# Routing tail and experts of a four-layer cross-attention stack: powers computed earlier, three scatters under way, two blocks made one

## Chip, cores and metric

The kernel runs on one core of one Trainium2 chip. The metric is the device time of one execution in microseconds; before the change it is 3072.48 us, the median of three runs (3069.31 to 3073.73).

## What is computed

A stack of four layers works on `x` (32 batches of 112 tokens, width 256, f32) with a context of 32 x 375 rows. Each layer adds a gated attention over the context and a gated second part: mixture of experts, a searched network, a ternary product, a routed layer. The change touches only the first layer:

```python
x = x + tanh(g_xattn[0]) * attention0(layernorm(x), ctx, pad_mask)
x = x + tanh(g_ffn[0])   * mixture0(layernorm(x))
# mixture0, on N = 3584 tokens, 8 experts of capacity 1024:
probs = softmax(x @ Wr);  w_topk, e_topk = top_k(probs, 2)
pos   = place of each (token, choice) in its expert's queue, in token order
buf   = zeros(8, 1024, 256).at[e_flat, pos].set(x_rep, mode='drop')
h     = rms(buf, norm_w);  buf_out = (gelu(h @ Wg) * (h @ Wu)) @ Wd + buf
combined = x + sum over 2 choices of w_topk * buf_out[e, pos]
fout  = gelu(rms(x) @ fWg) * (rms(x) @ fWu) @ fWd + x     # shared, small
out   = where(a choice overflowed its expert, fout, combined)
```

## The kernel before, in words

`first_attention` (L209) is one block: five instruction streams, one for each engine, that meet at a barrier when it ends. It walks the 32 batches in a software pipeline; batches are also four groups of eight (`G = 8`) for the routing. For each group TensorE makes the router's logits, VectorE multiplies them by the tokens' inverse size (`token_shift`, L1329, which waits for `r_invs_done`), ScalarE takes the exponential, VectorE picks the two best experts (`token_pick`), TensorE counts places (`token_places`, L1368), and VectorE turns them into row numbers (`token_rows`, L1381, which raises `put_ready`). GpSimd then writes the group's rows into a queue in HBM by 16 indirect transfers (`token_scatter`, L1398), each of up to 112 rows of 1 KB.

The inverse sizes come from GpSimd: `token_half_scales` (L1229), `token_sizes` (L1238) and `token_inverses` (L1248), which are powers of the variances.

After the last attention batch comes the tail, in four functions. `shared_scatters` (L1451) is GpSimd's: the scatters of groups 2 and 3 (`LAST - 1` and `LAST`), with a wait for the landing of all so far after each fourth, and group 3's sizes after the fourth scatter of group 2, its inverses after the eighth. `shared_vectors` (L1467), `shared_scalars` and `shared_products` (L1550) are the shared expert for all eight half groups (`gate_and_up(n)`, `gelu(n)`, `hide(n)`, `down(n)`, `add_shared(n)`), with group 3's routing written into that order by hand: VectorE does `hide(1)`, `add_shared(0)`, `token_shift(3)`, `token_pick(3)`, `hide(2)`, `add_shared(1)`, `token_rows(3)`, and so on; ScalarE takes group 3's exponential ahead of `gelu(2)`; TensorE does `route_rows`, `gate_and_up(2)`, `down(1)`, `gate_and_up(3)`, `token_places(3)`, `down(2)`, and so on. The last `add_shared` raises `added` to 32.

Then the block ends: every engine drains, they meet, the semaphores are cleared. `run_experts` (L1630) is the next block: 16 units of 512 queue rows, two to an expert. Weights of expert 0 are there by then; the slots of experts 1 and 2 lie where the attention's tiles lay. SyncE loads the rows of units 0 and 1 (512 KB each), then six weight transfers of 512 KB (experts 1 and 2), then goes on unit by unit. GpSimd starts five small loads. TensorE transposes unit 0's rows as soon as they are in, and from there products of 128x512 follow each other.

Once the experts are done, `gathered_attention` (the second layer's attention, which also fetches the experts' output rows) and the rest follow; nothing of them is changed.

Of the kernel before, what the change touches and what calls it, by code (L numbers as in the profile page):

```python
# [13 lines left out]
P = 128  # L14
# [40 lines left out]
def row(v):  # L55

    return v.rearrange("(a n) -> a n", a=1)
# [151 lines left out]
def first_attention(k, m, t):  # L209
# [4 lines left out]
    with nc.cleanup_on_exit():  # L214
        w = Fields()
# [35 lines left out]
        ctx_loaded = [sem(nc, f"ctx{j}_loaded") for j in range(NB)]  # L251
# [5 lines left out]
        shared_storage(k, q, w.pad, s)  # L257

        with nc.Block() as block:
            @block.sync  # L260
            def _(sp):
                opening_loads(k, w, o, sp)
                sp.wait_ge(o.s["zeros_ready"], 1)
                for j in range(CT, B):
                    sp.wait_ge(s["scores_done"], j - CT + 1)
                    sp.dma_start(w.ctx_t[:, j % CT, :, :], k.ctx_t_dram[j]).then_inc(w.ctx_t_loaded[j % CT], 16)
                    if j == 2 * CT:
                        for t, src in ((m.f_norm[:, :], (k.inputs["L0_ffn_f_norm"])), (m.fwg[:, :, :], k.inputs["L0_ffn_fWg"]),
                                       (m.fwu[:, :, :], k.inputs["L0_ffn_fWu"]), (m.fwd[:, :], k.inputs["L0_ffn_fWd"]),
                                       (m.wr[:, :, :], k.inputs["L0_ffn_Wr"])):  # L270
                            sp.dma_start(t, src).then_inc(m.s["shared_loaded"], 16)
# [9 lines left out]
                for j in range(NB):  # L281
                    sp.wait_ge(ctx_loaded[j], 16 * (B // NB))

            @block.gpsimd
            def _(pool):
# [68 lines left out]
                shared_scatters(k, m, t, pool)  # L354

            @block.vector
            def _(dve):
# [101 lines left out]
                shared_vectors(k, m, t, q, dve, PLACES)  # L459

            @block.scalar
            def _(act):
# [76 lines left out]
                shared_scalars(k, t, q, act)  # L539

            @block.tensor
            def _(pe):
# [62 lines left out]
                def attend(j):  # L605
                    u = j % 2
                    if j < NB:
                        pe.wait_ge(k.ctx_first[j], 16)
                    else:
                        pe.wait_ge(ctx_loaded[j % NB], 16 * (j // NB))  # L610
# [48 lines left out]
                shared_products(k, m, t, q, pe, PLACES)  # L659

# [596 lines left out]
def routing_storage(k, w, net):  # L1257
# [48 lines left out]
    t.scattered = [sem(nc, f"scattered{g}") for g in range(B // G)]  # L1306
# [91 lines left out]
def token_scatter(k, t, pool, g, n):  # L1398

    j, r = divmod(n, TOP_K)  # L1400
    if n == 0:
        pool.wait_ge(t.s["put_ready"], g + 1)
    pool.indirect_dma_start(k.queue[:, :], bass.IndirectOffsetOnAxis(ap=t.put_at[:, g, r, j:j + 1], axis=0), t.xr[g][:, j, :], None,
                            bounds_check=ROWS - 1, oob_is_err=False).then_inc(t.scattered[g], 16)
# [43 lines left out]
LAST = B // G - 1  # L1448


def shared_scatters(k, w, t, pool):  # L1451

    token_half_scales(k, w, pool, GH * (LAST + 1) - 1)
    for g in (LAST - 1, LAST):
        for n in range(G * TOP_K):
            token_scatter(k, t, pool, g, n)
# [173 lines left out]
def run_experts(k, w, net):  # L1630

    nc = k.nc
    UNITS_E = CAPACITY // UR
    N = E * UNITS_E
    with nc.cleanup_on_exit():
        rows = sb(nc, "rows", [P, 2, TILES, D], F32)
        rows_t = sb(nc, "rows_t", [P, 2, DC, UR], F32)
        gated = sb(nc, "gated", [P, 2, UR], F32)
        hidden = sb(nc, "hidden", [P, 2, FC, UR], F32)
        out = sb(nc, "out", [P, 2, TILES, D], F32)  # L1640
        rows_in = [sem(nc, f"rows{u}_in") for u in range(N)]
        rows_out = [sem(nc, f"rows{u}_out") for u in range(N)]
        names = "transposed rows_copied gate_done gated_done up_done hidden_done down_done out_copied"
        s = {n: sem(nc, n) for n in names.split()}
        RT, GATE, UP, DOWN = 0, 2, 4, 6

        with nc.Block() as block:
            @block.sync
            def _(sp):
                for u in range(N + 2):  # L1650
                    if u < N:
                        if u >= 2:
                            sp.wait_ge(s["transposed"], u - 1)
                        sp.dma_start(rows[:, u % 2, :, :], k.queue[u * UR:(u + 1) * UR, :].rearrange("(p t) d -> p t d", p=P)).then_inc(rows_in[u], 16)
# [3 lines left out]
                    if u >= 2:  # L1658
                        sp.wait_ge(s["out_copied"], 2 * (u - 1))
                        sp.dma_start(k.outputs[(u - 2) * UR:(u - 1) * UR, :].rearrange("(p t) d -> p t d", p=P), out[:, u % 2, :, :]).then_inc(rows_out[u - 2], 16)  # L1660
                    e, last = divmod(u - 1 - UNITS_E, UNITS_E)
                    if last == 0 and 0 <= e < E - EXPERT_RING:
                        sp.wait_ge(s["down_done"], 2 * UNITS_E * (e + 1))
                        load_expert(k, w, sp, e + EXPERT_RING)
                    if last == 0 and e == E - 2:
                        sp.wait_ge(s["down_done"], 2 * UNITS_E * (e + 1))
                        for q in range(EARLY_EDGES):
                            c, i = divmod(q, 3)
                            sp.dma_start(early_edge(w, q), k.we_t_dram[searched_edges()[c][i][0]]).then_inc(w.early_loaded[q], 16)
                    for n in range(2 * (u - 2), min(2 * (u - 1), 5 * NODES)):  # L1670
                        if u >= 2:
                            net.load_raw(sp, n)
                for u in range(N):
                    sp.wait_ge(rows_out[u], 16)

            @block.gpsimd
            def _(pool):
                for t, name in ((net.ew[:, :], "L1_ffn_ew"), (net.act_w[:, :], "L1_ffn_act_w")):
                    pool.dma_start(t, k.inputs[name].rearrange("c i -> (c i)" if name == "L1_ffn_ew" else "c -> c").rearrange("(a n) -> a n", a=1).partition_broadcast(P)).then_inc(net.s["scalars_loaded"], 16)
                pool.dma_start(net.be[:, :, :], k.inputs["L1_ffn_be"]).then_inc(net.s["scalars_loaded"], 16)  # L1680
                pool.dma_start(net.gamma[:, :], row(k.inputs["L1_ffn_ln_g"]).partition_broadcast(S)).then_inc(net.s["rows_loaded"], 16)
                pool.dma_start(net.beta[:, :], row(k.inputs["L1_ffn_ln_b"]).partition_broadcast(S)).then_inc(net.s["rows_loaded"], 16)
                pool.wait_ge(net.s["scalars_loaded"], 48)
                for c, edges in enumerate(searched_edges()):
                    for i in range(3):
                        pool.tensor_scalar(net.be_s[:, c, i, :], net.be[:, edges[i][0], :], net.ew[:, 3 * c + i:3 * c + i + 1], None, ALU.mult).then_inc(net.s["be_scaled"], 1)
                pool.wait_ge(net.s["rows_loaded"], 32)
                pool.tensor_scalar(net.gamma[:, :], net.gamma[:, :], k.tg[0:S, 5:6], None, ALU.mult).then_inc(net.s["rows_scaled"], 1)
                pool.tensor_scalar(net.beta[:, :], net.beta[:, :], k.tg[0:S, 5:6], None, ALU.mult).then_inc(net.s["rows_scaled"], 1)
                for c in range(NODES):  # L1690
                    pool.wait_ge(net.raw_loaded[c], 80)
                    pool.tensor_scalar(net.wq[:, c, :, :], net.wq[:, c, :, :], net.ew[:, 3 * c:3 * c + 1], None, ALU.mult).then_inc(net.s["ends_scaled"], 1)
                    pool.tensor_scalar(net.wo[:, c, :, :], net.wo[:, c, :, :], net.act_w[:, c:c + 1], None, ALU.mult).then_inc(net.s["ends_scaled"], 1)
                pool.wait_ge(net.s["ends_scaled"], 2 * NODES)
                pool.wait_ge(net.s["rows_scaled"], 2)
                pool.wait_ge(net.s["be_scaled"], 3 * NODES)

            @block.scalar
            def _(act):
                def copy_rows(u):  # L1700
                    if u == 0:
                        act.wait_ge(w.s["norms_loaded"], 16 * E)
                    act.wait_ge(s["transposed"], u + 1)
                    if u >= 2:
                        act.wait_ge(s["up_done"], (u - 1) * FC)
                    for c in range(DC):
# [1858 lines left out]
```

## Time and profile before

| | |
|---|---|
| median of three runs | 3072.48 us (3069.31 to 3073.73) |
| span of the profiled execution | 3069.1 us |
| TensorE busy / granted clock over the span | 96% / 0.973 |
| tail of the first block (last attention batch to last `added`) | about 203 to 277.5 us |
| first block's end to first transpose of the experts | 277.5 to 290.6 us |
| experts' block | 290.6 to 644 us |

The profiled execution comes with no time other than its span; the span lies 0.2 us under the fastest of the three runs and 3.4 us under their median. A granted clock of 1.0 is TensorE's full clock of 2.4 GHz, 0.5 is 1.2 GHz. All times inside the kernel are counted from the span's start.

### The profile page before, as it was taken

What the parts mean: (1) busy time and instruction counts of PE and PEld (TensorE: products, weight loads), DVE (VectorE), ACT (ScalarE), POOL (GpSimd) and SP (SyncE); (2) the same over time, 40 slices, a digit from 0 to 9 for tenths busy, and PEclk for the clock granted to TensorE, in tenths of its full rate; (3) what the DMA queues carried; (4) which work ended last, traced back from release to release, by engine and by line L of the source; (5) the groups of instructions that cost most, each with busy time, mean ns of one, the idle gap of its engine ahead of it and who ended that gap; (6) DMA issues with size and microseconds to landing.
All of it is one profiled execution on the core that took longest, in us unless ns stands there. A gap on an engine that the chain in (4) does not pass through costs nothing. (4 is left out here: it accounts for less than half of the span.)

```text
span 3069.1 us, 61161 instructions
## 1 busy us (share of the span) xinstructions
PE 2945.7 (96%) x23332; PEld 2275.7 (74%) x23332; DVE 2030.9 (66%) x4378; ACT 1448.5 (47%) x2845; POOL 650.4 (21%) x952
## 2 busy tenths in 40 slices
PE   8997999989899999999999999799999999899999
PEld 6874656567799999999999999577777777556444
DVE  5773111138577887788888877566767666589664
ACT  3431111126455555555555555476666666556000
POOL 4565000046100220013012200212212112036000
PEclk9997999999899999999999999899999999899999
DMA  9643233249300000000000000000000000337100
GB/s 292 214 128 106 82 117 110 88 144 299 104 1 2 1 2 1 2 1 1 2 1 2 1 2 1 24 25 22 17 22 22 17 22 17 106 108 227 51 14 21
DMA packets 79537, 185.47 MB, mean 60 GB/s; under 512 B 12981, under 2 KB 23202, under 8 KB 78916
## 3 DMA queue, kind: packets, MB, share of 16 engines
q1 hardware_dynamic: 62708, 141.50, 14.3%
q10 hardware_dynamic: 10208, 25.30, 2.8%
q0 software_dynamic: 6336, 14.76, 1.7%
q8 instruction: 192, 3.15, 0.4%
q14 instruction: 93, 0.76, 0.1%
HBM read 150.26 MB, written 27.79 MB: 58 GB/s over the span
## 5 line engine op out<-in xcount | busy, mean ns | idle before, releaser
L2792 DVE CUSTOM_DVE_ANT_0 probs<-ps,add 112x375 f32<-112x375 f32 x512 | 258.9, 544 | 82.7 <-PE ps L2945 76.0
L2871 ACT ACTIVATE probs<-probs,neg_top 112x375 f32<-112x375 f32 x512 | 278.5, 600 | 63.5 <-DVE neg_top L2792 60.1
L1734 DVE TENSOR_TENSOR hidden<-gated,ps 128x512 f32<-128x512 f32 x64 | 44.0, 687 | 294.7 <-PE ps L1777 294.7
L2972 PEld LDWEIGHTS ps<-ident,probs 112*125 112x125 f32 x1536 | 196.8, 188 | 44.4 <-issue 16.7
L2351 DVE TENSOR_REDUCE top<-ps 112x16 f32<-112x1792 f32 x96 | 194.2, 2023 | 46.1 <-PE ps L2590 45.9
L2972 PE MATMUL ps<-ident,probs 112*125 112x112 f32 x1536 | 219.7, 279 | 1.8 <-DVE probs_t L2799 1.8
L3416 PE MATMUL ps<-we,xn_t 128*128 128x512 f32 x448 | 201.9, 614 | 1.7 <-PEq L846 0.9
L2367 DVE TENSOR_TENSOR probs<-probs,inv_sum 112x1792 f32<-112x1792 f32 x96 | 196.0, 2042 | 3.3
L2355 DVE TENSOR_TENSOR probs<-ps,top 112x1792 f32<-112x1792 f32 x96 | 194.3, 2024 | 3.3
L2363 DVE TENSOR_REDUCE row_sum<-probs 112x16 f32<-112x1792 f32 x96 | 193.9, 2020 | 3.2 <-ACT probs L2475 3.2
L2558 PE MATMUL ps<-ident,probs 112*112 112x112 f32 x1536 | 179.8, 260 | 8.2 <-ACT probs_t L2470 7.3
L2799 DVE COPY probs_t<-ps 125x336 f32<-125x336 f32 x256 | 129.5, 506 | 83.0 <-PE ps L2972 83.0
L2470 ACT ACTIVATE probs_t<-ps 112x896 f32<-112x896 f32 x192 | 176.1, 917 | 15.2 <-PE ps L2558 3.7
L2549 PE MATMUL ps<-wv,nodes 128*112 128x256 f32 x768 | 181.4, 379 | 0.0
L2558 PEld LDWEIGHTS ps<-ident,probs 112*112 112x112 f32 x1536 | 162.2, 134 | 25.8 <-issue 7.9
L2344 DVE COPY v<-ps 112x512 f32<-112x512 f32 x96 | 66.3, 691 | 169.4 <-PE ps L2549 169.4
L2573 PE MATMUL ps<-nodes,wq 128*128 128x224 f32 x768 | 178.1, 354 | 0.1
L2575 PE MATMUL ps<-att_t,wo 128*128 128x224 f32 x768 | 176.6, 352 | 0.0
L2525 PE MATMUL ps<-nodes,wkh 128*128 128x224 f32 x768 | 171.8, 367 | 0.0
L1715 ACT ACTIVATE gated<-ps 128x512 f32<-128x512 f32 x64 | 38.2, 597 | 282.8 <-PE ps L1772 282.8
L3416 PEld LDWEIGHTS ps<-we,xn_t 128*128 128x128 f32 x448 | 87.8, 197 | 112.8 <-issue 98.8
L2475 ACT ACTIVATE probs<-probs 112x1792 f32<-112x1792 f32 x96 | 162.9, 1697 | 7.1 <-DVE probs L2355 7.0
(464 smaller groups left out, 6276.8 us busy)
## 6 DMA issues: line engine op xcount, KB each, us to landing
ctx_t<-in_ctx_T_dram SPq DMA_DIRECT2D x96, 375.0 KB, 4.5
ctx_sb<-in_ctx_dram ACTq DMA_DIRECT2D x64, 384.0 KB, 4.5
ctx_sb<-in_ctx_dram SPq DMA_DIRECT2D x32, 384.0 KB, 8.9
ctx_sb<-in_ctx_T_dram SPq DMA_DIRECT2D x32, 375.0 KB, 3.1
queue<-zeros SPq DMA_DIRECT2D x32, 256.0 KB, 5.1
rows<-queue SPq DMA_DIRECT2D x16, 512.0 KB, 4.9
outputs<-out SPq DMA_DIRECT2D x16, 512.0 KB, 2.9
mask_in<-in_mask_BxSxS_fk_dram SPq DMA_DIRECT2D x16, 328.1 KB
```

The lines of the kernel that those rows point to most:

```text
L2351: dve.tensor_reduce(top[:, :, :], scores, AX.X, ALU.max).then_inc(s["top_done"], 1)
L2355: dve.tensor_tensor(probs[:, m % 2, :, :, :], scores, top[:, :, :].unsqueeze(3).broadcast_to([S, 4, PAIR * HQ, S]), ALU.subtract).then_inc ...
L2363: dve.tensor_reduce(row_sum[:, :, :], p, AX.X, ALU.add).then_inc(s["sum_done"], 1)
L2367: dve.tensor_tensor(p, p, inv_sum[:, :, :].unsqueeze(3).broadcast_to([S, 4, PAIR * HQ, S]), ALU.mult).then_inc(s["probs_normed"], 1)
L2549: mm = pe.matmul(k.ps[0:S, ODD, b * D:(b + 1) * D], node_v[:, i, b * S:(b + 1) * S], w.wv[:, c, i, :], start=i == 0, stop=i == DC - 1)
L2558: mm = pe.transpose(k.ps[0:S, PT + h // 4, h % 4 * S:(h % 4 + 1) * S], probs[:, m % 2, h % 4, b * HQ + h // 4, :], k.ident[0:S, 0:S])
L2573: pe.matmul(k.ps[:, EVEN, a * PS:(a + 1) * PS], w.wq[:, c, i, cut], node_q[:, i, :], start=i == 0, stop=False)
L2575: mm = pe.matmul(k.ps[:, EVEN, a * PS:(a + 1) * PS], w.wo[:, c, i, cut], att_t[:, i, :], start=False, stop=i == DC - 1)
L2792: dve.tensor_tensor_reduce(out=probs[:, u, h, :], in0=k.ps[0:S, SCORE + h, 0:L], in1=add[:, j % 2, :], scale=1.0, scalar=BIG, op0=ALU.add, ...
L2871: act.activation(probs[:, u, h, :], probs[:, u, h, :], ACT.Exp, bias=neg_top[:, u, h:h + 1], scale=-1.0).then_inc(s["probs_done"], 1)
L2972: mm = pe.transpose(k.ps[0:KR, PT + h % 2, r * S:(r + 1) * S], probs[:, n % 3, h, r * KR:(r + 1) * KR], k.ident[0:S, 0:S])
L3416: mm = pe.matmul(k.ps[:, Y + at % YB, :], xn_t[:, c, (j + u) * P:(j + u + 1) * P], r.we[:, c, e:e + TWO, :].rearrange("p e d -> p (e d)"), ...
```

## The change

1. `shared_scatters` computes group 3's sizes and inverses before the first of its scatters.
2. The 32 scatters of groups 2 and 3 count on three semaphores in turn (`UNDER_WAY = 3`); scatter i waits for the landing of scatter i - 3, where before each fourth waited for all. Scatters of groups 0 and 1 keep their semaphores.
3. `first_attention` and `run_experts` become one block. The experts' tiles are allotted over the attention's, from the same base. Each engine's expert stream begins with a wait for `added` = 32. GpSimd no longer waits at the end for the last scatters; SyncE does, ahead of the first load of rows.
4. SyncE's order changes: after `added` it issues the six transfers of experts 1 and 2, then waits for the scatters, then loads the rows of units 0 and 1. Semaphores of the units' transfers are two and two instead of sixteen and sixteen, and the attention's context semaphores are the ones that the first loads used.

```diff
 def first_attention(k, m, t, net):
+        ex = Fields()
+        base = nc.sbuf_base
+        experts_storage(k, m, ex)
+        top = nc.sbuf_base
+        nc.sbuf_base = base
...
-        ctx_loaded = [sem(nc, f"ctx{j}_loaded") for j in range(NB)]
+        ctx_loaded = k.ctx_first
...
+        nc.sbuf_base = max(top, nc.sbuf_base)
...
+                experts_loads(k, m, net, ex, t, q, sp)      # end of SyncE's stream
+                experts_scales(k, net, q, pool)             # end of GpSimd's
+                experts_vectors(k, ex, q, dve)              # end of VectorE's
+                experts_scalars(k, m, ex, q, act)           # end of ScalarE's
+                experts_products(k, m, ex, q, pe)           # end of TensorE's
...
+UNDER_WAY = 3
 def shared_scatters(k, w, t, pool):
     token_half_scales(k, w, pool, GH * (LAST + 1) - 1)
-    for g in (LAST - 1, LAST):
-        for n in range(G * TOP_K):
-            token_scatter(k, t, pool, g, n)
-            if g == LAST - 1 and n == 3:
-                token_sizes(k, w, pool, LAST)
-            elif g == LAST - 1 and n == 7:
-                token_inverses(k, w, pool, LAST)
-            if n % 4 == 3:
-                pool.wait_ge(t.scattered[g], 16 * (n + 1))
-    for g in range(LAST + 1):
-        pool.wait_ge(t.scattered[g], 16 * G * TOP_K)
+    token_sizes(k, w, pool, LAST)
+    token_inverses(k, w, pool, LAST)
+    count = 2 * G * TOP_K
+    for i in range(count):
+        g, n = divmod(i, G * TOP_K)
+        if i >= UNDER_WAY:
+            pool.wait_ge(t.landed[i % UNDER_WAY], 16 * (i // UNDER_WAY))
+        token_scatter(k, t, pool, LAST - 1 + g, n, t.landed[i % UNDER_WAY])
...
+def experts_loads(k, w, net, x, t, q, sp):
+    sp.wait_ge(q.s["added"], B)
+    for e in range(1, EXPERT_RING):
+        load_expert(k, w, sp, e)
+    for g in range(LAST - 1):
+        sp.wait_ge(t.scattered[g], 16 * G * TOP_K)
+    for i in range(UNDER_WAY):
+        sp.wait_ge(t.landed[i], 16 * len(range(i, 2 * G * TOP_K, UNDER_WAY)))
+    for u in range(N + 2):
+        if u < N:
+            if u >= 2:
+                sp.wait_ge(s["transposed"], u - 1)
+            sp.dma_start(x.rows[:, u % 2, :, :], k.queue[u * UR:(u + 1) * UR, :]...).then_inc(x.rows_in[u % 2], 16)
...
-                    if u == 1:
-                        for e in range(1, EXPERT_RING):
-                            load_expert(k, w, sp, e)
```

The rest of the experts' streams is the old code, moved into functions.

## Rows read from the trace of the kernel before

**Rows 1.** Head of the page: span, and busy time of the engines.
```profile
span 3069.1 us, 61161 instructions
...
PE 2945.7 (96%) x23332; PEld 2275.7 (74%) x23332; DVE 2030.9 (66%) x4378; ACT 1448.5 (47%) x2845; POOL 650.4 (21%) x952
```

**Rows 2.** Stretches of five us: busy time of the engines, granted clock, DMA share, GB/s.
```profile
230.00:235.00 5.00, 5.00 (x13) 2.46 (x13) 0.00 (x0) 0.00 (x0) 3.75 (x5) 0.66 0.17 52
235.00:240.00 5.00, 1.95 (x9) 1.24 (x7) 0.76 (x4) 0.37 (x2) 4.07 (x5) 1.00 0.19 58
240.00:245.00 5.00, 3.22 (x5) 1.53 (x6) 4.72 (x36) 1.72 (x2) 3.11 (x4) 0.61 0.29 89
...
295.00:300.00 5.00, 5.00 (x8) 2.05 (x7) 0.00 (x0) 0.60 (x1) 3.92 (x16) 0.58 1.03 362
300.00:305.00 5.00, 5.00 (x19) 2.69 (x18) 1.38 (x2) 0.60 (x1) 2.62 (x6) 1.00 0.65 256
```

**Rows 3.** Timeline of VectorE in the tail (start, duration, line, idle before).
```profile
227.64 1.65 DVE L1489 SCALAR_TENSOR_TENSOR x_sb<-ps,wo,x_sb 112x256 f32<-112x256 f32 x4
238.85 0.22 DVE L1334 TENSOR_TENSOR wo<-ps,r_inv 112x64 f32<-112x64 f32 x1 [9.56 <-POOL r_inv L1254]
...
243.67 0.61 DVE L1479 TENSOR_TENSOR pad<-gated,ps 128x448 f32<-128x448 f32 x1
...
249.83 0.22 DVE L1385 TENSOR_SCALAR wo<-ps 112x64 f32<-112x64 f32 x1 [3.97 <-PE ps L1376]
...
275.76 1.74 DVE L1489 SCALAR_TENSOR_TENSOR x_sb<-ps,wo,x_sb 112x256 f32<-112x256 f32 x4 [0.41 <-PE ps L1604]
```

**Rows 4.** Timeline of TensorE, the tail and the start of the experts.
```profile
227.20 3.22 PE L1576 MATMUL ps<-wr,last_t 128*112 128x8 f32 x32
...
235.06 1.89 PE L1604 MATMUL ps<-fwd,pad 128*112 128x256 f32 x8
241.78 3.36 PE L1590 MATMUL ps<-wv,fwg 128*128 128x448 f32 x4 [4.83 <-issue]
244.93 3.18 PE L1590 MATMUL ps<-wv,fwu 128*128 128x448 f32 x4
...
251.44 1.67 PE L1590 MATMUL ps<-wo,fwg 128*128 128x448 f32 x4
...
290.61 1.97 PE L1747 MATMUL ps<-ident,rows 128*128 128x128 f32 x8 [14.03 <-DMA rows<-queue]
```

**Rows 5.** Timeline of GpSimd in the tail.
```profile
224.56 1.05 POOL L1403 DMA_INDIRECT queue<-wkh,wo  x1 [3.86 <-DVE wo L1395]
...
236.77 1.69 POOL L1252 TENSOR_TENSOR rstd<-var_eps,neg_half 112x8 f32<-112x8 f32 x1
...
250.12 0.94 POOL L1403 DMA_INDIRECT queue<-wkh,wo  x1 [0.30 <-issue]
253.45 0.94 POOL L1403 DMA_INDIRECT queue<-wv,wo  x1 [2.39 <-DMA queue<-wkh,wo]
...
278.25 0.94 POOL L1403 DMA_INDIRECT queue<-wv,wo  x1 [0.31 <-issue]
```

**Rows 6.** Sequencer instructions at the first block's end (duration ns min/median/max, start us).
```profile
L259 POOLq COMPARE_BRANCH  x1: 38/38/38, 280.7 to 280.7; - x1
L259 POOLq DRAIN  x1: 5291/5291/5291, 280.9 to 280.9; - x1
```

**Rows 7.** Timeline of SyncE's queue at the start of the experts.
```profile
287.26 0.81 SPq L1654 DMA_DIRECT2D rows<-queue  x2
...
290.76 0.50 SPq L2153 DMA_DIRECT2D wd<-in_L_ffn_Wd_dram  x1
```

**Rows 8.** Issues at 287.26, 288.12 and 290.76: KB, us from issue to landing.
```profile
rows<-queue SPq DMA_DIRECT2D x1, 512.0 KB, 3.3
...
wg<-in_L_ffn_Wg_dram SPq DMA_DIRECT2D x1, 512.0 KB, 7.2
...
wd<-in_L_ffn_Wd_dram SPq DMA_DIRECT2D x1, 512.0 KB, 13.1
```

More of the change, by code:

```diff
@@ L1305, in routing_storage @@
     t.s = {n: sem(nc, n) for n in names.split()}
-    t.scattered = [sem(nc, f"scattered{g}") for g in range(B // G)]
+    t.scattered = [sem(nc, f"scattered{g}") for g in range(LAST - 1)]
+    t.landed = [sem(nc, f"landed{i}") for i in range(UNDER_WAY)]
     t.steps = 0
@@ new lines, in experts_storage @@
+    for _ in range(1, EXPERT_RING):
+        expert_slot(k, w)
+    x.rows = sb(nc, "rows", [P, 2, TILES, D], F32)
+    x.rows_t = sb(nc, "rows_t", [P, 2, DC, UR], F32)
+    x.gated = sb(nc, "gated", [P, 2, UR], F32)
+    x.hidden = sb(nc, "hidden", [P, 2, FC, UR], F32)
+    x.out = sb(nc, "out", [P, 2, TILES, D], F32)
+    x.rows_in = [sem(nc, f"rows{u}_in") for u in range(2)]
+    x.rows_out = [sem(nc, f"rows{u}_out") for u in range(2)]
+    names = "transposed rows_copied gate_done gated_done up_done hidden_done down_done out_copied"
@@ new lines, in experts_scalars, with copy_rows @@
+def experts_scalars(k, w, x, q, act):
+    s = x.s
+    N = UNITS_ALL
+    act.wait_ge(q.s["added"], B)
+    def copy_rows(u):
+        if u == 0:
+            act.wait_ge(w.s["norms_loaded"], 16 * E)
+        act.wait_ge(s["transposed"], u + 1)
+        if u >= 2:
+            act.wait_ge(s["up_done"], (u - 1) * FC)
+        for c in range(DC):
+            ins = act.activation(x.rows_t[:, u % 2, c, :], k.ps[:, RT + c, :], ACT.Copy, scale=w.norm[:, u // UNITS_E, c:c + 1])
+        ins.then_inc(s["rows_copied"], 1)
+    copy_rows(0)
+    for n in range(N * FC):
+        act.wait_ge(s["gate_done"], n + 1)
+        if n >= 2:
+            act.wait_ge(s["hidden_done"], n - 1)
+        act.activation(x.gated[:, n % 2, :], k.ps[:, GATE + n % 2, :], ACT.Gelu).then_inc(s["gated_done"], 1)
+        if n % FC == 2 and n // FC + 1 < N:
+            copy_rows(n // FC + 1)
@@ new lines, in experts_vectors, with copy_out @@
+def experts_vectors(k, x, q, dve):
+    s = x.s
+    N = UNITS_ALL
+    dve.wait_ge(q.s["added"], B)
+    def copy_out(u):
+        if u >= 2:
+            dve.wait_ge(x.rows_out[u % 2], 16 * (u // 2))
+        for b in range(2):
+            dve.wait_ge(s["down_done"], 2 * u + b + 1)
+            dve.tensor_copy(x.out[:, u % 2, 2 * b:2 * b + 2, :], k.ps[:, DOWN + b, :].rearrange("p (t d) -> p t d", t=2)).then_inc(s["out_copied"], 1)
+    for n in range(N * FC):
+        u, f = divmod(n, FC)
+        dve.wait_ge(s["gated_done"], n + 1)
+        dve.wait_ge(s["up_done"], n + 1)
+        if u >= 2 and f == 0:
+            dve.wait_ge(s["down_done"], 2 * (u - 1))
+        dve.tensor_tensor(x.hidden[:, u % 2, f, :], x.gated[:, n % 2, :], k.ps[:, UP + n % 2, :], ALU.mult).then_inc(s["hidden_done"], 1)
+        if f == 1 and u:
+            copy_out(u - 1)
+    copy_out(N - 1)
@@ L2160, in early_edge @@
     return home[:, q % 2 * DC * D:(q % 2 + 1) * DC * D].rearrange("p (c d) -> p c d", c=DC)
-def mixture_of_experts(k, w, net):
-    nc = k.nc
-    with nc.cleanup_on_exit():
-        for _ in range(1, EXPERT_RING):
-            expert_slot(k, w)
-        run_experts(k, w, net)
 H2, HD2 = 16, D // 16
```

253 lines of the change are left out of this document (100 added, 153 removed).

## The prediction, made before the result was known

> **What bounds the kernel now.** I read the head of the page first: TensorE is busy for 96% of the span [rows 1], so what can be won lies in the few places where it stands still. The change touches only the stretch from the last attention batch to the experts' first product, so I then read five-us stretches of it [rows 2]: TensorE is busy 1.95 of 5 us at 235 to 240, and 3.22 at 240 to 245. The timelines name the two stalls. The first is a chain: VectorE ends `add_shared(0)` at 229.3 and cannot start group 3's routing before 238.85, since GpSimd's inverse sizes come last, 9.56 us of idle [rows 3]. Behind it ScalarE's exponential and `gelu(2)`, and so TensorE's `gate_and_up(3)`, start late: 4.83 us of idle before 241.78 [rows 4]. The second stall is the change of block. VectorE's last addition ends at 277.5 [rows 3], TensorE's first transpose starts at 290.61, after 14.03 us of idle, when the rows of unit 0 land [rows 4]: 13.1 us. They consist of the last scatters (issued at 278.25 [rows 5], landed by about 280.7, when GpSimd leaves its last wait [rows 6]), a drain of GpSimd of 5.29 us [rows 6], some 1.1 us of barriers and clearing up to SyncE's first issue at 287.26 [rows 7], and 3.3 us of transfer [rows 8]. From 290.61 on the experts are bound by TensorE, as is most of what follows, so a shift of that first transpose reaches the end of the kernel whole. What I forecast is this one number.
>
> **Part 1, the early powers.** GpSimd stands still for 3.86 us before its scatter at 224.56, from 220.70 on, until group 2's row numbers are ready [rows 5]. The powers (two of 1.69 us, as the one at 236.77 [rows 5]; with two short operations and waits, for which I allow 0.8 us, some 4.2 together) go there and end at about 224.9. The first scatter then starts at about 225.4 instead of 224.56: 0.8 us later, and off the path, as part 2 shows. VectorE's `token_shift(3)` no longer waits for them; what is late next are the logits. TensorE ends `route_rows` at 230.42 [rows 4], so `token_shift(3)` starts at 230.5, 8.35 us earlier. From there to the start of `hide(2)` took 4.82 us (238.85 to 243.67 [rows 3]): `hide(2)` at 235.3, its product ready (`gate_and_up(2)` is done when `down(1)` starts, 235.06 [rows 4]), done at 235.9. `gelu(2)` is done by about 233.6. TensorE ends `down(1)` at 236.95 [rows 4] and goes straight on with `gate_and_up(3)`, 4.83 us earlier.
>
> How long that takes depends on the clock. Before, it ran after the idle at the low level: 3.36 and 3.18 us for two products of four [rows 4], granted clock 0.61 in 240 to 245 [rows 2]. The same products took 1.67 us at full clock (251.44 [rows 4]). With no idle ahead, and the granted clock at 1.00 in 235 to 240 [rows 2], I take full clock: from the start of one to what follows the other 3.0 us instead of 6.1. `token_places(3)` then starts at 239.9 instead of about 247.9, and VectorE's `token_rows(3)` at 241.8 instead of 249.83 [rows 3]: 8.0 us earlier. From there to the end of the tail the order and its waits are unchanged, at full clock but for one short dip that stays. The tail ends 8.0 us earlier, at 277.5 - 8.0 = 269.5. Bounds: if the clock stays low, 3.3 us of it are lost (4.8 won, the idle alone); the logits allow no more than 8.35.
>
> **Part 2, three scatters under way.** Before, four scatters take 7.08 us (three steps of 1.25 us and one of 3.33, 250.12 to 253.45 [rows 5]), 1.77 each. A scatter whose landing is waited for lets the next start 3.33 us after its own start; with three under way that bound is 3.33 / 3 = 1.11 us, less than the 1.25 us that GpSimd needs to issue one. So I take 1.25 us each. The extra wait instruction is not in the trace; between 0 and 0.5 us each, I take nearly 0, since it mostly finds its count reached. Last scatter: 225.4 + 31 x 1.25 = 264.2 (group 3's row numbers are ready at about 243.8, its first scatter's turn comes at 245.4, so nothing is waited for), landed 2.45 us later (as 278.25 to 280.7 [rows 5, 6]): 266.6. That is ahead of `added` at 269.5 and also at 1.4 us each (271.3) it is ahead of the first load of rows. GpSimd is off the path. This part gains nothing by itself, but without it the scatters would end at 225.4 + 54.9 + 2.45 = 282.7 and be last.
>
> **Part 3, one block.** The drain, the barriers and the clearing (280.7 to 287.26, 6.6 us) go. What starts next is SyncE's queue at `added`, 269.5 + 0.1 = 269.6. The other engines' waits for `added` hold nothing that could run earlier: TensorE, ScalarE and VectorE need the rows, GpSimd's five small loads are needed only in the next block.
>
> **Part 4, SyncE's order.** Here the gain of part 3 is given back. Ahead of the rows of unit 0 now stand six transfers of 512 KB. In the trace rows 0 landed 3.3 us after the first issue at 287.26, at 290.6, and the eighth transfer, `wd` of expert 2, at 290.76 + 13.1 = 303.9 [rows 7, 8]: landings come in the order of issue (`wg` of expert 1, the third, at 288.12 + 7.2 = 295.3), seven of them in 13.3 us, 1.90 us each with GpSimd's 256 KB among them. Now rows 0 are the seventh transfer: 3.3 + 6 x 1.90 = 14.7 us after the first issue. So the first transpose starts at 269.6 + 14.7 = 284.3. Bounds: at 362 GB/s, the best stretch [rows 2], six transfers and 256 KB (3.4 MB) take 9.4 us instead of 11.4, start at 282.3; at 2.2 us each, 286.1. The clock costs the same as before: TensorE stands still for some 15 us, as before for 14, and starts at the low level (0.58 still at 295 to 300, 1.00 from 300 [rows 2]); when it is released may differ by a us or two either way.
>
> The Trainium skill ("DMA: Bandwidth & Descriptors", Specifications) puts the limit of HBM for a core at about 358 GB/s; by it the queue would need 9.5 us for those 3.4 MB and the kernel would come to 3064.3 us. The trace reaches 362 GB/s in one stretch and 256 in the next [rows 2], so I keep the landings' own pace.
>
> **Sum.** First transpose from 290.6 to 284.3: 6.3 us less, 8.0 from the tail, 1.7 lost because `added` to first transpose grows from 13.1 to 14.8. The experts themselves, their end and all behind keep their durations: the same instructions in the same order. Fewer semaphores are cleared at one end instead of two, below 0.4 us. Span 3069.1 - 6.3 = 3062.8; the median of the runs lies 3.4 us above the profiled span, so 3072.5 - 6.3 = 3066.2 us.
>
> **Rivals.**
> - *Scatters become the bound (the slower side).* A wait before each scatter might keep GpSimd from preparing the next one, so that issue and landing follow each other. It takes the place of the drain as what SyncE waits for. It decides from the pace at which rows 0, issued at the last landing, come as late as before: 290.6 - 3.3 - 2.45 = 284.9 for the last start, (284.9 - 225.4) / 31 = 1.92 us each. At 2.2 us: last start 293.6, landed 296.1, rows 299.4, 8.8 us later: 3081 us. Fully one after another (3.33) it is 3116. Against it: steps of 1.25 us in one group of four and three allowed in flight. Chance 0.04. In its mild form, the old pace of 1.77, the scatters land at 282.7 and the rows at 286.0: 3067.9 us, 0.09.
> - *The clock stays low over `gate_and_up(3)`.* The stretch before it has small products of eight columns, after which the granted clock was 0.66 at 230 to 235 [rows 2]. Then 3.3 us are lost: 3069.5 us. Against it, 1.00 from 235 on. Chance 0.12.
> - *Rows overtake the weights.* If the 16 DMA engines served the transfers side by side, rows 0 would land 3.3 us after their issue, that is 269.6 + 3.1 + 3.3 = 276.0, 14.6 us earlier: 3057.9 us. Against it, landings in order of issue [rows 8]. Chance 0.05. The Trainium skill ("DMA: Bandwidth & Descriptors", Queues, rings and completion order) says that each DMA engine consumes a queue's descriptors in ring order; by that rule this rival is out, and the trace agrees.
> - *Weights come faster.* At 362 GB/s throughout: 3064.2 us. For it that stretch; against it the slower ones at both sides. Chance 0.20.
>
> **How the numbers follow.** My forecast, 3066.2 us, has 0.50, and around each case I allow 1.5 us for the median of a few runs and for the clock's release. About 0.2% of 3072.5 us, 6.1 us, is what a measurement of this kernel can tell from no change; the border is 3066.3. Faster by more: half of the forecast with a little (0.27), most of the faster weights (0.18) and the overtaking rows (0.05), 0.50. Slower by over 0.2%: 0.04, the scatters. The rest, 0.46, lies within. The range 3062.5 to 3069.8 takes in the faster weights, the mild scatters and the low clock, and leaves out the overtaking and the slow scatters and some scatter of the runs.
>
> **What would show each step.** Part 1: VectorE's wait before `token_shift(3)` shrinks from 9.6 to about 1 us and names TensorE, and `gate_and_up(3)` takes 3.2 us, not 6.5. Part 2: GpSimd's indirect transfers 1.25 us apart, last start near 264. Part 3: no drain between the last scatter and the experts. Part 4: six weight transfers issued from about 269.6, the first transpose near 284.3, its wait put down to the rows, 14 to 15 us after `added`. A first transpose before 280 or after 288 would prove a step wrong, as would a different length from there to the end.

## The result, and the profile after

After the change the kernel takes 3090.85 us (median of four runs, 3090.03 to 3094.62), beside it the kernel before 3073.11 us (four runs, 3069.31 to 3075.07): a ratio of 1.0066, 95% interval 1.0054 to 1.0078. It became slower by some 18 us; I had forecast 3066.2 us. The profiled execution has a span of 3089.4 us against 3069.1 [rows 1], at a granted clock of 0.969 against 0.973.

The head of the page shows no new work (TensorE 2955.8 us busy against 2945.7, VectorE 2032.5 against 2030.9), so the loss is idle time and slow clock:

```profile
span 3089.4 us, 61118 instructions
...
PE 2955.8 (96%) x23332; PEld 2281.4 (74%) x23332; DVE 2032.5 (66%) x4378; ACT 1448.4 (47%) x2845; POOL 647.7 (21%) x952
```

The stretches of five us that answer to [rows 2] show where. From 235 to 250 TensorE works 5.4 of 15 us, and its clock is at the lower level from 240 to 260; a second hole is at 275 to 285. The clock fell there after TensorE had stood still (1.03 of 5 us busy in 235 to 240).

```profile
230.00:235.00 5.00, 5.00 (x11) 2.43 (x11) 0.46 (x3) 0.00 (x0) 3.78 (x5) 0.66 0.30 92
235.00:240.00 5.00, 1.03 (x5) 0.53 (x3) 2.62 (x26) 1.54 (x2) 3.78 (x5) 1.00 0.30 93
240.00:245.00 5.00, 2.14 (x3) 1.17 (x4) 0.26 (x2) 0.54 (x1) 3.24 (x4) 0.52 0.30 93
245.00:250.00 5.00, 2.27 (x4) 0.65 (x3) 2.69 (x10) 0.54 (x1) 0.00 (x0) 0.50 0.02 6
250.00:255.00 5.00, 5.00 (x21) 3.74 (x19) 0.45 (x2) 0.00 (x0) 0.00 (x0) 0.50 0.01 3
255.00:260.00 5.00, 5.00 (x13) 3.63 (x14) 4.02 (x15) 0.00 (x0) 1.36 (x2) 0.50 0.04 11
...
275.00:280.00 5.00, 2.21 (x8) 1.09 (x6) 0.00 (x0) 0.00 (x0) 2.68 (x3) 1.00 0.21 63
```

GpSimd's timeline (answers to [rows 5]) does what was forecast: powers over by 223.87, sixteen scatters 1.25 us apart, then group 3's. But that second run starts after 14.18 us of idle, since VectorE's row numbers are not there:

```profile
223.67 0.20 POOL L1262 TENSOR_TENSOR r_inv<-r_inv,rstd 112x8 f32<-112x8 f32 x1
224.40 1.05 POOL L1412 DMA_INDIRECT queue<-wkh,wo  x1 [0.53 <-issue]
225.76 0.96 POOL L1412 DMA_INDIRECT queue<-wkh,wo  x1 [0.30 <-issue]
...
243.22 0.94 POOL L1412 DMA_INDIRECT queue<-wkh,wo  x1 [0.30 <-issue]
258.34 0.94 POOL L1412 DMA_INDIRECT queue<-wv,wo  x1 [14.18 <-DVE wo L1404]
...
277.35 0.94 POOL L1412 DMA_INDIRECT queue<-wv,wo  x1 [0.30 <-issue]
```

VectorE's timeline (answers to [rows 3]) holds the cause. In brackets stands the idle time before the instruction and what the profile names as its end; "remote" and "issue" name no engine's work.

```profile
234.47 0.23 DVE L1343 TENSOR_TENSOR wo<-ps,r_inv 112x64 f32<-112x64 f32 x1 [6.29 <-remote]
...
237.58 0.16 DVE L1366 FIND_INDEX8 wo<-wo 112x8 uint32<-112x8 f32 x1
237.66 0.07 DVE L1366 MATCH_VALUE_LOAD wo<-wo 112x8 f32 x1
238.71 0.17 DVE L1366 FIND_INDEX8 wo<-wo 112x8 uint32<-112x8 f32 x1 [0.96 <-issue]
238.79 0.07 DVE L1366 MATCH_VALUE_LOAD wo<-wo 112x8 f32 x1
239.44 0.17 DVE L1366 FIND_INDEX8 wo<-wo 112x8 uint32<-112x8 f32 x1 [0.56 <-issue]
240.84 0.09 DVE L1366 MATCH_VALUE_LOAD wo<-wo 112x8 f32 x1 [1.23 <-issue]
242.24 0.17 DVE L1366 FIND_INDEX8 wo<-wo 112x8 uint32<-112x8 f32 x1 [1.31 <-issue]
247.21 0.20 DVE L1368 CAST wo<-wo 112x64 f32<-112x64 uint32 x1 [4.80 <-remote]
...
255.52 0.23 DVE L1394 TENSOR_SCALAR wo<-ps 112x64 f32<-112x64 f32 x1 [5.07 <-PE ps L1385]
...
280.35 0.88 DVE L1496 SCALAR_TENSOR_TENSOR x_sb<-ps,wo,x_sb 112x256 f32<-112x256 f32 x2 [6.84 <-remote]
...
290.06 1.74 DVE L1496 SCALAR_TENSOR_TENSOR x_sb<-ps,wo,x_sb 112x256 f32<-112x256 f32 x4 [0.41 <-PE ps L1611]
```

The eight searches of L1366 wait for nothing but each other, and five of them go at 0.14 us each. Then VectorE crawls (0.96, 0.56, 1.23, 1.31 us between instructions) and stands still for 4.80 us. That is no wait of the program. ScalarE stops too, with its input ready. `gelu(2)`, at 242.26, needs a gate product that was done at 232.11 (TensorE's L1597, 229.35 + 2.76); once its activation table was loaded at 236.80, all 5.46 us are a stop. The gate product for the `gelu` at 281.10 ended at 274.85 (272.05 + 2.80, last line below), so at least 6.2 of its 14.36 us are a stop; the rest was waiting for input.

```profile
235.52 1.28 ACT L1544 ACT_TABLE_LOAD   x1
242.26 0.54 ACT L1544 ACTIVATE gated<-ps 128x448 f32<-128x448 f32 x1 [5.46 <-remote]
...
281.10 0.54 ACT L1544 ACTIVATE gated<-ps 128x448 f32<-128x448 f32 x1 [14.36 <-remote]
...
272.05 2.80 PE L1597 MATMUL ps<-last_t,fwg 128*128 128x448 f32 x4
```

A rival that the trace itself can settle is that the engines wait for their own code to be loaded. Between 219.5 and 253 us, in which three of these stops end, the profile has packets of GpSimd's queue alone and none of the two queues that it calls "instruction"; between 271.5 and 290 us it has none of theirs either. So no arriving code ends the stops.

```profile
q0 software_dynamic: 768, 1.84, 17.8%
```

All of this lies while GpSimd issues one indirect transfer behind another (224 to 244, 258 to 278), and TensorE (answers to [rows 4]) pays for it:

```profile
226.27 3.22 PE L1583 MATMUL ps<-wr,last_t 128*112 128x8 f32 x32
...
242.86 3.35 PE L1597 MATMUL ps<-wv,fwg 128*128 128x448 f32 x4 [6.83 <-issue]
248.94 3.35 PE L1597 MATMUL ps<-wv,fwu 128*128 128x448 f32 x4 [2.73 <-DVE pad L1486]
...
281.28 2.05 PE L1611 MATMUL ps<-fwd,pad 128*112 128x256 f32 x4 [4.06 <-DVE x_sb L1496]
...
306.80 1.94 PE L1780 MATMUL ps<-ident,rows 128*128 128x128 f32 x8 [15.91 <-DMA rows<-queue]
```

SyncE's queue (answers to [rows 7, 8]) issues the six weights from 291.90 and the rows at 295.11, which land 11.6 us later. The drain that stood at 280.9 [rows 6] now stands at the end of the merged block, where SyncE is not done before 659.8:

```profile
L265 POOLq DRAIN  x1: 5707/5707/5707, 652.4 to 652.4; - x1
```

The next block's first product is at 661.25 us against 645.25 before, 16.0 us later. The other four of the 20.3 us of the span arise 30 us behind it, in code that nothing changed: TensorE stands still for 3.96 us before 692.15, and the ten us around that run at 0.51 of the clock (first fence). Before, the answering stretch (second fence) held 0.83. VectorE had waited 3.04 us for gathered rows there, against 1.39 before. This can't be laid to the change: two executions of one and the same kernel below (e11 and e15) show both forms.

```profile
691.20:701.20 10.00, 6.98 (x17) 4.51 (x18) 7.76 (x23) 5.65 (x14) 8.40 (x12) 0.51 0.53 159
```

```profile
675.20:685.20 10.00, 6.87 (x28) 5.28 (x29) 6.77 (x21) 5.72 (x13) 8.26 (x11) 0.83 0.47 141
```

### The profile page after: what moved, and what is told of

Same layout as the page of the kernel before. It is cut to its first block and busy times, and to the rows that moved or that the text cites. A ratio compares the mean times of both kernels' runs of the same rounds, so it can differ in the third digit from the quotient of the medians.

```text
span 3089.4 us, 61118 instructions
## 1 busy us (share of the span) xinstructions
PE 2955.8 (96%) x23332; PEld 2281.4 (74%) x23332; DVE 2032.5 (66%) x4378; ACT 1448.4 (47%) x2845; POOL 647.7 (21%) x952
## 3 DMA queue, kind: packets, MB, share of 16 engines
q1 hardware_dynamic: 62708, 141.50, 14.4%
```

## Experiments

Theory A: a long run of indirect transfers, each issued as soon as GpSimd can, stops VectorE and ScalarE. Rival B: the merged block itself (other places, other semaphores) does. Rival C: the early powers do. In the table, "stops" are gaps above 2 us put down to "remote" between 215 and 295 us (VectorE's, ScalarE's; a gap can hold some time in which the input wasn't ready either), "T" is the first transpose of the experts. Ratios are to runs of the kernel before on the same chip. The end of group 3's router products (`route_rows`) lies anywhere from 222 to 233 us in these executions, and 4.2 us apart in two of the same kernel; so T is compared between kernels by the last column, the time from that end to T. It is 60.2 us before (230.42 to 290.61), and the forecast was 53.9 (230.42 to 284.3).

| run | median us | ratio, 95% interval | stops V / S, us | T, us | router to T, us |
|---|---|---|---|---|---|
| after | 3090.85 | 1.0066 (1.0054 to 1.0078) | 6.3 4.8 6.8 / 5.5 14.4 | 306.80 | 77.3 |
| e1_batches | 3067.11 | 0.9988 (0.9977 to 0.9999) | none | 285.87 | 58.0 |
| e2_three_alone | 3068.84 | 0.9993 (0.9981 to 1.0005) | 4.7 4.9 / 10.1 | 285.44 | 56.5 |
| e3_powers_alone | 3074.32 | 1.0012 (0.9999 to 1.0024) | none | 294.92 | 61.6 |
| e4_rows_first | 3067.45 | 0.9981 (0.9972 to 0.9991) | none | 283.34 | 55.8 |
| e5_two | 3072.13 | 1.0004 (0.9992 to 1.0016) | none | 284.75 | 58.2 |
| e6_paced_early | 3067.13 | 0.9985 (0.9973 to 0.9997) | none | 280.69 | 58.5 |
| e7_no_rows | 3087.92 | 1.0046 (1.0030 to 1.0062) | 8.4 2.4 / 3.3 14.7 | 307.64 | 74.9 |
| e8_eights | 3068.84 | 0.9987 (0.9977 to 0.9998) | 6.6 4.5 / - | 284.39 | 57.3 |
| e9_pow_between | 3075.47 | 1.0007 (0.9997 to 1.0017) | 3.7 2.0 6.4 / 7.1 | 289.04 | 59.5 |
| e10_direct | 3067.45 | 0.9985 (0.9975 to 0.9995) | none | 282.19 | 51.1 |
| e11_short_pause | 3055.95 | 0.9945 (0.9929 to 0.9962) | none | 278.12 | 52.2 |
| e12_pause_alone | 3069.51 | 0.9998 (0.9989 to 1.0006) | 4.8 / 9.8 6.0 | 284.80 | 56.2 |
| e13_no_rows_first | 3063.11 | 0.9978 (0.9968 to 0.9988) | none | 281.71 | 54.9 |
| e14_group1_only | 3067.16 | 0.9992 (0.9981 to 1.0004) | 3.4 2.1 / 16.4 8.0 | 282.37 | 54.8 |
| e15_short_pause_again | 3059.36 | 0.9953 (0.9940 to 0.9965) | none | 281.74 | 51.6 |

**e1_batches**: the kernel after, with the old pacing of the scatters.

```diff
-        if i >= UNDER_WAY:
-            pool.wait_ge(t.landed[i % UNDER_WAY], 16 * (i // UNDER_WAY))
         token_scatter(...)
+        if i % 4 == 3:                       # all issued so far have landed
+            for v in range(UNDER_WAY):
+                pool.wait_ge(t.landed[v], 16 * len(range(v, i + 1, UNDER_WAY)))
```

> The changed kernel with one part undone: scatters of groups 2 and 3 again in batches of four, all landed before the next batch. Theory A (a stream of indirect transfers without a pause freezes VectorE and ScalarE for some 5 us at a time, which the trace of the changed kernel calls remote): no freezes, VectorE's last addition near 269, last scatter starts near 277.7 (224.4 and 53.3 us for eight batches), landed 280.2, rows 0 in and first transpose near 284, 6 to 7 us earlier than before: about 3067 us. Rival B (the one block itself, its longer instruction streams, brings the freezes): freezes stay, about 3090 us.

Some 24 us come back, the time is the forecast one, and block, powers and load order are those of the change: neither B nor C is enough for the stops. VectorE goes through group 3's routing without one, and `gate_and_up(3)` (last line) runs at full clock:

```profile
228.63 0.22 DVE L1343 TENSOR_TENSOR wo<-ps,r_inv 112x64 f32<-112x64 f32 x1 [2.09 <-PE ps L1584]
...
239.15 0.23 DVE L1394 TENSOR_SCALAR wo<-ps 112x64 f32<-112x64 f32 x1 [3.57 <-PE ps L1385]
...
234.26 1.67 PE L1598 MATMUL ps<-wv,fwg 128*128 128x448 f32 x4
```

**e2_three_alone** and **e3_powers_alone**: the kernel before with one part each, three under way in place of batches of four, and the powers ahead of the scatters.

> The kernel before with one part of the change alone: three scatters of groups 2 and 3 under way, the powers and the two blocks as they were. Theory A: VectorE and ScalarE freeze as in the changed kernel, the tail ends 5 to 15 us later than before and the kernel takes 3078 to 3090 us. Rival B: no freezes; the scatters end some 10 us earlier and with them, bounded by the additions at 277.5, the block: 3069 to 3072 us.

> The kernel before with the early powers alone. Theory A and my working of part 1: VectorE's wait for r_inv goes from 9.6 to about 1 us, gate_and_up(3) runs at full clock, the last addition ends near 269.5, 8 us earlier; but the scatters in batches end at 225.4 + 53.3 = 278.7 instead of 278.25, and they then set the block's end: 3072 to 3074 us. Rival C (the early powers, beside VectorE's routing, cause the freezes): freezes of 5 us in VectorE between 228 and 250, the tail ends later than before.

Three under way bring the stops with them into the kernel before, so B and C aren't needed for them either. The time was a miss: 3078 to 3090 us had been forecast. There GpSimd's powers stand between the scatters (runs of 4, 4, 8 and 16), and the last scatter starts at 271.11 instead of 278.25, which wins about what the stops lose. The powers alone do end VectorE's wait for them (2.3 us of idle, now for TensorE, where 9.56 stood [rows 3]); the last addition ends at 272.42, and the scatters (last start 282.63) set the block's end. Part 2 had said that they would; all of this execution ran some 3 us late from the router on.

**e5_two**: `UNDER_WAY = 2` in the kernel after.

> The changed kernel with two scatters under way instead of three. The pace by landings is 3.33 / 2 = 1.67 us, so there is a pause of about 0.8 us after every second one. Theory A, if it is the missing pause that freezes: no freezes, last scatter starts at 224.4 + 31 x 1.67 = 276.2, landed 278.7, first transpose near 283: about 3066 us. If it is the number of transfers since the last standstill that counts, freezes stay: 3080 us or more. Rival B: freezes stay.

No stop, at a pace of about 1.66 us up to 266 us; the last four scatters then take 12 us, while the weights are on the way. The time is a miss: 3066 us had been forecast, and 3072.13 is no gain on the kernel before. That T, at 284.75, lies near the 284.3 forecast for three is luck: the router's products ended 3.9 us earlier in this execution.

**e7_no_rows**: the last 32 scatters with `bounds_check=0`, so that none but queue row 0 is written; the placing of groups 2 and 3 is left out.

> The changed kernel, in which the scatters of groups 2 and 3 drop every row except row 0 by their bounds (so those tokens' rows are not written to the queue): the same 32 indirect transfers at the same pace, with hardly any data. If GpSimd's own work on an indirect transfer freezes the other engines, VectorE and ScalarE freeze as in the changed kernel, the last addition ends near 290. If the transfers' traffic or their rows' landing does it, there are no freezes, and it ends near 269.

The stops stay (below, VectorE), with next to no bytes moved (below, 226 to 244 us: 0.01 MB, packets under 512 bytes). It isn't the rows' traffic. What is left is GpSimd's own work for an indirect transfer, and the small packets that go with each.

```profile
239.76 0.23 DVE L1343 TENSOR_TENSOR wo<-ps,r_inv 112x64 f32<-112x64 f32 x1 [8.35 <-remote]
...
275.83 0.88 DVE L1496 SCALAR_TENSOR_TENSOR x_sb<-ps,wo,x_sb 112x256 f32<-112x256 f32 x2 [2.43 <-remote]
```

```profile
DMA packets 576, 0.01 MB, mean 0 GB/s; under 512 B 576, under 2 KB 576, under 8 KB 576
```

**e10_direct**: the last 32 as plain transfers of the same 112 x 1 KB to consecutive queue rows, three under way; the placing by row number is left out.

> The kernel after the change, with the last 32 scatters issued as plain GpSimd transfers of the same 112 x 1 KB to consecutive queue rows, three under way as before; the placing of those rows by their row numbers is left out. If the stop of VectorE and ScalarE needs the indirect form (its addresses come from SBUF), the gaps go: last add 265 to 270 us, 3066 to 3070 us (0.998 to 0.9995). If any software transfer of GpSimd in an unbroken run does it, the gaps of 4 to 7 us stay and the time is 3085 to 3092 us (1.004 to 1.006).

No stop, and the time is in the range forecast for that; the bytes and the small packets are there, so they alone don't make a stop. But an issue takes 0.53 us in place of 0.94, and GpSimd then waits for landings, so that both the form and the pauses differ: this alone doesn't say which of them counts.

**e8_eights**, **e9_pow_between**, **e12_pause_alone**: how long a run, and what ends it. Batches of eight; in the kernel after, one small power after each fourth scatter; and in the kernel after, a short wait after each fourth:

```diff
+        if i % 4 == 3:
+            pool.wait_ge(t.landed[(i - 1) % UNDER_WAY], 16 * ((i - 1) // UNDER_WAY + 1))
```

> The changed kernel with the scatters in batches of eight, each batch landed before the next. If a run of eight at 1.25 us is long enough (as the run at 198 to 205 us and the run of eight in the kernel with three scatters alone suggest), VectorE or ScalarE freezes for some 5 us towards the end of a batch, in at least one of four batches, and the last addition ends 4 to 12 us later than with batches of four (265 to 269). If only longer runs do it, there are none and the scatters end at 224.4 + 4 x 12.1 = 272 before contention, the first transpose comes near 282.

> The kernel after the change, with a power of one column (about 0.7 us of GpSimd's own arithmetic) after every fourth of the last 32 scatters; all three stay under way and nothing waits for a landing more. Theory A (an unbroken run of indirect transfers stops VectorE and ScalarE until GpSimd does something else) has two readings. A1: any other instruction of GpSimd ends the run: then no gap of over 4 us on VectorE or ScalarE in 215 to 290 us, the last add at about 265 to 269 us, a median of 3066 to 3069 us (ratio 0.998 to 0.999). A2: only a pause for a landing ends it (what piles up is work of the queue that isn't done yet): then gaps of 4 to 7 us as after the change, the last add near 290 us, 3088 to 3091 us (1.005 to 1.006).

> The kernel after the change with one thing added: after each fourth of the last 32 scatters GpSimd waits until the one before it has landed (a pause of 1.14 us instead of 0.30, as e11_short_pause showed it). Nothing of group 1's scatters or of the loads' order is changed, so this tells what the short pause is worth by itself. Theory A: no gap of over 4 us on VectorE or ScalarE between 225 and 290 us (the one at about 206 us, of group 1's eight, stays), a pace of 1.46 us, the last scatter 46 us after the 33rd, the first transpose of gathered rows 50 to 56 us after the router's logits begin, the next block's first product at 634 to 639 us, 3058 to 3066 us (ratio 0.9955 to 0.9975). Rival (e11's time comes from group 1's batches and the rows loaded first, or from the sum of them): 3066 to 3070 us (0.998 to 0.999), as e1_batches.

Eight in a row are enough for a stop (first line below: 6.61 us, ended at 232.31 as the batch ended at 231.07 + 0.94), as forecast; the last addition came 4.1 us later than with batches of four. In e9 arithmetic of GpSimd between the scatters doesn't end a run: A2 for the first sixteen; the second sixteen passed without a stop, and 3075.47 us lies between the two forecasts, so neither reading holds for all. The short pause (1.14 us of GpSimd idle, second line) alone was a miss: the stops returned (lines after it), and the time with them, 3069.51 us where 3058 to 3066 had been forecast.

```profile
232.31 0.22 DVE L1343 TENSOR_TENSOR wo<-ps,r_inv 112x64 f32<-112x64 f32 x1 [6.61 <-remote]
```

```profile
229.37 0.94 POOL L1412 DMA_INDIRECT queue<-wkh,wo  x1 [1.14 <-DMA queue<-wkh,wo]
...
243.32 0.22 DVE L1394 TENSOR_SCALAR wo<-ps 112x64 f32<-112x64 f32 x1 [4.80 <-remote]
```

```profile
204.91 0.36 ACT L508 ACTIVATE att_t<-ps 128x224 f32<-128x224 f32 x1 [5.36 <-remote]
247.77 0.54 ACT L1546 ACTIVATE gated<-ps 128x448 f32<-128x448 f32 x1 [9.83 <-remote]
```

The line at 204.91 is one that the kernel before has too (below): group 1 has eight scatters close together there, the last six of them some 1.25 us apart, and the last ends at 203.5.

```profile
206.98 0.36 ACT L499 ACTIVATE att_t<-ps 128x224 f32<-128x224 f32 x1 [5.37 <-remote]
```

**e4_rows_first**, **e6_paced_early**, **e11_short_pause**: towards a better kernel. e4 is e1 with the rows of units 0 and 1 loaded ahead of the six weights; e6 breaks up group 1's last eight: a wait for the first eight, and one of GpSimd's small powers (`token_half_scales`) moved ahead by two scatters; e11 takes e6's full landing after each fourth of the last 32 back to the short wait above (without the wait for i - 3).

```diff
+                pool.wait_ge(t.scattered[1], 16 * 8)        # e6, ahead of group 1's ninth
                 scatter(B)
+                token_half_scales(k, m, pool, GH * LAST)
                 scatter(B + 1)
                 pool.wait_ge(t.scattered[1], 16 * 12)
-                token_half_scales(k, m, pool, GH * LAST)
```

> The changed kernel with scatters in batches of four and with the rows of units 0 and 1 loaded ahead of the six weight transfers. In the kernel with batches alone the weights were issued while the last eight scatters were still to come, and one batch took 6.7 us instead of 3.3 to land. If the weights' traffic did that, all batches now take 3.3 us, the last landing and the first transpose come 3.3 us earlier than in the kernel with batches alone, and the kernel takes about 3.5 us less than that one. If not, the two kernels take the same time.

> The kernel with batches and rows first, and with the last eight scatters of group 1 too (the run at 198 to 205 us that all kernels have) cut into batches of four by waits. Theory A (a long run of indirect transfers at 1.25 us freezes ScalarE and VectorE): ScalarE's idle of 5.4 us before its copy of att_t at 207 falls to about 2, TensorE's 3.6 us of idle before 207.4 goes, group 2's scatters start 2 to 3 us earlier, and with them the end: 2 to 4 us less than with rows first alone. Rival (that idle has another cause): it stays, and the added waits cost 0 to 3 us.

> Batches of four and group 1's last eight in batches too (as in e6_paced_early), but the pause after each fourth of the last 32 scatters waits only for the landing of the one before the last, not of the last. Theory A (a pause of the run of some length is what matters): if a pause of about 1 us is enough, no gap of over 4 us, the pace falls from 1.8 to about 1.45 us, the last scatter starts near 266 us instead of 274.6, and 3064 to 3067 us (ratio 0.997 to 0.9985), as far as the weights' issue is what sets the block's end. If the whole landing is needed, one to three gaps of 4 to 7 us come back and the last add moves to 270 to 285 us, 3069 to 3082 us. Rival (the block's end doesn't hang on the pause): no difference from e6 (0.9985) either way.

e4 wins 2.5 us at T and nothing that the medians show. In e6 no stop is left anywhere, the one at 204 is gone too; but its time, 3067.13 us, is e4's, and the 2 to 4 us forecast were not won. e11 has no stop either and issues four scatters in 5.83 us instead of 7.1:

```profile
228.56 0.94 POOL L1413 DMA_INDIRECT queue<-wkh,wo  x1 [0.30 <-issue]
230.64 0.94 POOL L1413 DMA_INDIRECT queue<-wkh,wo  x1 [1.13 <-issue]
```

It is the fastest, and faster than forecast: 3055.95 us, and 3059.36 us in a second set of runs (e15, 3054.11 to 3066.05); the two intervals end at 0.9962 and 0.9965.

**e13_no_rows_first**, **e14_group1_only**, **e15_short_pause_again**: e11 without the order of loads; e11 without the pause (three under way); e11 itself.

> e11_short_pause without the order of loads (the six weights go ahead of rows 0 again): group 1's last eight scatters in batches of four, and the pause of 1.14 us after each fourth of the last 32. If what went before decides (an unbroken eight of group 1 leaves something behind): no gap over 4 us on VectorE or ScalarE between 195 and 290 us, the first transpose 2.5 us later than in e11 because of the weights, 3057 to 3062 us (ratio 0.9955 to 0.997). If the load order decided, or the pause is at the edge by itself: gaps as in e12_pause_alone, 3066 to 3071 us (0.998 to 1.0).

> e11_short_pause without the pause: group 1's last eight in batches and the rows loaded first, but the last 32 scatters with three under way, as in the kernel after. If the last 32's own unbroken run is what stops the engines: gaps of 4 to 7 us from about the sixth scatter of the run on, the first transpose past 298 us, 3080 to 3090 us (ratio 1.003 to 1.0055). If what went before decides: none, 3052 to 3060 us (0.993 to 0.996).

> e11_short_pause again, beside kernels that differ from it by one edit each. If its time is the kernel's own: 3054 to 3060 us, ratio 0.993 to 0.9965, no gap over 4 us between 195 and 290 us. If it sits at an edge that one execution falls over and another not: 3060 to 3070 us or a spread over both.

With both (group 1 broken up, and the pause) no stop comes, in two kernels and three executions (e11, e13, e15). With the pause alone (e12) there are three, with group 1 alone (e14) four, ScalarE's longest 16.4 us. So both runs seem to count, though group 1's eight end 20 us before the last 32 begin, with four more scatters and GpSimd's powers between: as if something were left behind that a short pause doesn't clear. That isn't shown: these are single profiled executions, and with full landings (e1, e4) or two under way (e5) the last 32 pass without a stop though group 1's eight are unbroken. e12 also keeps the wait for i - 3, which e11 and e13 lack, but its scatters start at the same steps as theirs. e14 was forecast at 3080 to 3090 us and took 3067.16, since it has the rows first: its last addition ends late, at 277.97, but T follows in 4.4 us, where the kernel after needs 15.0. Here and in e13 against e15 (3.75 us between the medians, ratios on the same chip whose intervals just don't overlap) the order of loads shows its worth.

## Why the prediction was wrong, step by step

The step that failed is "GpSimd is off the path" in part 2: it put the cost of the unbroken scatters for the other engines at nothing. The stops that came in its place show in part 1's terms, as 22.3 us.

- **Part 1** is where the time was lost. It said "`token_shift(3)` starts at 230.5", from there the old durations, and "the tail ends 8.0 us earlier, at 277.5 - 8.0 = 269.5". The logits were ready at 229.49, one us ahead of that; VectorE started at 234.47, had its row numbers' input at 255.52 instead of 241.8 (13.7 us late: 4.0 at the start, 9.0 in the searches, the rest on TensorE at the low clock), and the last addition ended at 291.80 (another 8.6 us, 6.84 of them one stop). 22.3 us in sum. That the stops are the cause is shown by e1, which takes them away and nothing else but the pacing. The dependencies were read rightly: where the stops are away (e1) `token_shift(3)` is at 228.63, `token_rows(3)` 10.5 us behind it (forecast 11.3), the last addition at 265.19. `gate_and_up(3)` at full clock was right for e1 too (1.67 us at 234.26), and wrong after (3.35 us for each half, granted clock 0.50 to 0.52), since TensorE had stood still ahead of it.
- **Part 2** had the pace (1.25 us) and the powers right, and the conclusion "GpSimd is off the path" wrong. It took the engines for independent of each other but for semaphores, so a gapless stream could cost nothing. The old pacing, read only as lost time (a step of 3.33 us after each fourth), was what kept the other engines going. The trace of before had the warning: ScalarE's 5.37 us before 206.98, in the middle of group 1's scatters, which fall to 2.15 us where these are broken up (e6). I had not looked at that stretch, since the change doesn't touch it.
- **Part 3** was right: drain and barriers are off the path.
- **Part 4** was right, for the reason given: first transpose 15.0 us after the last addition, forecast 14.8; the rows follow the six weights. The rivals on the weights and on overtaking were settled by this.
- **Sum.** Of the profiled span, 22.3 us are missed in the tail, 0.2 in part 4, and some 4 us in `gathered_attention`, which the sum held fixed. The last belong to the execution and not to the change: that block's sixth score product starts 46.5 us after its first product before and 50.0 after, but also 45.7 in e11 and 49.6 in e15, one kernel twice. What makes a gather late was not tried.
- **Rivals.** The slower side was there with 0.04, by a mechanism (pace above 1.92 us) that the runs rule out: the pace was 1.25. The low clock over `gate_and_up(3)` did come, but as a consequence of the stops. None of the rivals was what happened: one engine's stream stopping others with which it shares no semaphore.

What the stop itself is stays open. The Trainium skill ("SBUF — State Buffer", Who interferes with whom) knows a lock between VectorE and GpSimd and says that ScalarE has ports of its own; here ScalarE stood still as well, so that rule alone doesn't explain it. That the unbroken stream of indirect transfers brings the stops is shown (after, e1, e2), and that the rows' bytes aren't needed (e7); that the indirect form is needed is not (e10).

## What to carry to other kernels

A stream of GpSimd's indirect transfers isn't free for the other engines even where nobody waits for it: break it after each fourth, in this kernel by a us or more of standing still and all along, and read VectorE's and ScalarE's timelines during such a run before its pauses are taken out. A gap put down to "remote" or "issue", between instructions that wait for nothing, is not a wait of the program; where one stands in the trace of before, the change that lengthens its neighbourhood will have more of them. When an old pacing looks like waste, try it in small steps: here three in flight without a pause lost 18 us, and the kernel with a short pause after each fourth, group 1 broken up and the rows loaded first gained 12 to 17 us on the kernel before.

## What the runs showed of the hardware that I had not expected

- Eight to sixteen indirect GpSimd transfers 1.25 us apart stop VectorE and ScalarE for 4 to 7 us at a time (gaps up to 16 us), and TensorE keeps its pace until its inputs fail (5.00 of 5 us in 230 to 235, kernel after). There the first stop has begun by the fifth transfer of the first sixteen (logits ready at 229.49, VectorE idle), the one in the second sixteen only after the twelfth (VectorE idle from 273.51). With two under way, mostly 1.66 us apart, no stop came in 32; with 1.46 us apart it came in one kernel (e12) and not in two others (e11 and e13).
- A drain of GpSimd took about 0.08 us for each transfer it had issued since the last drain: 5.29 us after 64 [rows 6], 5.71 us after 69, and 0.46 us after 5 (kernel before, line below). Cutting a block in two doesn't make it longer; it only decides where it is paid.

```profile
L1647 POOLq DRAIN  x1: 457/457/457, 636.2 to 636.2; - x1
```
